# Attention and mixture-of-experts layer on one core: the two halves of the score banks in opposite phase, and each engine's order rearranged around it

## The reference, cut to what matters

```python
h = layernorm(x)
q, k, v = heads(h @ Wq + bq), heads(h @ Wk + bk), heads(h @ Wv + bv)      # 16 heads of 8
y  = softmax(causal(q k^T / sqrt(8))) v
qc = heads(h @ Wcq + bcq); kc, vc = heads(ctx @ Wck + bck), heads(ctx @ Wcv + bcv)
y += softmax(qc kc^T / sqrt(8)) vc
x  = x + y @ Wp + bp
f = layernorm(x)
shared = (silu(f @ w1.T) * (f @ w2.T)) @ w3s.T                             # hidden 512
gates  = sigmoid(f @ router.T), kept for the 2 largest of score + bias, of 8 experts
routed = sum over experts of gate * (silu(f @ a_e.T) * (f @ b_e.T)) @ w3_e.T   # hidden 128 each
out = x + shared + routed
```

## Time and profile before

| | |
|---|---|
| median of 3 runs | 439.8 us (433.45, 439.8, 442.03) |
| the profiled execution, its own time | 441.91 us |
| its span, first to last instruction | 440.2 us |
| TensorE busy | 396.3 us (90%) |
| VectorE busy | 353.5 us (80%) |
| ScalarE busy | 196.4 us (45%) |
| GpSimd busy | 77.8 us (18%) |
| TensorE clock granted, mean | 0.969 |

### The profile page before, as it was taken

One profiled execution on the slowest core, in us unless ns is written; L12 is line 12 of the kernel. 1 busy time (PEld: TensorE's weight loads), 2 busy tenths in 40 slices (PEclk: granted clock), 3 DMA queues, 4 the chain that ended last, 5 costly groups with the idle time before them and its releaser, 6 DMA issues.

```text
span 440.2 us, 10391 instructions
## 1 busy us (share of the span) xinstructions
PE 396.3 (90%) x3735; PEld 295.5 (67%) x3735; DVE 353.5 (80%) x1186; ACT 196.4 (45%) x326; POOL 77.8 (18%) x139
## 2 busy tenths in 40 slices
PE   0569998999989999999999999999989999998986
PEld 0447665666767676777677676767677766765985
DVE  4477776655889889897898888997989889884877
ACT  5135554432544544445534554455443554455221
POOL 4011001300221120311032022212031003201110
PEclk9999999755999999999999999999999999999999
DMA  5621102100021102011111102110101101000000
GB/s 135 211 99 47 61 14 75 54 19 18 20 67 37 50 20 83 12 42 48 46 38 54 48 6 77 42 36 24 72 6 52 43 27 48 1 24 1 2 13 12
DMA packets 28479, 19.63 MB, mean 45 GB/s; under 512 B 6681, under 2 KB 26273, under 8 KB 28449
## 3 DMA queue, kind: packets, MB, share of 16 engines
q1 hardware_dynamic: 27296, 19.02, 13.2%
q10 hardware_dynamic: 1152, 0.20, 0.3%
HBM read 5.58 MB, written 1.05 MB: 15 GB/s over the span
## 4 chain that ended last, share of the span: by engine, by line
PE 51%; DVE 29%; ACT 9%; issue 7%; DMA 1%; SPq 1%; DVEq 0%; POOL 0%; POOLq 0%; ACTq 0%
DVE masked_s L1045 9%; PE Y L579 9%; PE Bk L431 9%; PE Cb L431 7%; ACT probs L804 5%; PE S L455 4%; PE A L431 4%; DVE act L926 3%; DVE shifts L1051 3%; PE S L473 3%; PE Y L546 3%; DVE acc L966 2%; PE S L431 2%; PE Cb L662 2%; DVE qs L1018 2%
## 5 line engine op out<-in xcount | busy, mean ns | idle before, releaser
L804 ACT ACTIVATE probs<-S 128x1024 f32<-128x1024 f32 (+1 forms) x128 | 111.7, 917 | 47.2 <-PE S L457 46.2
L1045 DVE CUSTOM_DVE_ANT_0 masked_s<-S,later_keys 128x256 f32<-128x256 f32 (+1 forms) x256 | 74.1, 353 | 5.0 <-PE S L469 4.8
L1051 DVE TENSOR_REDUCE shifts<-S 128x4 f32<-128x1024 f32 x64 | 75.4, 1218 | 2.4 <-PE S L473 2.0
L791 ACT COPY yT<-Y 128x256 f32<-128x256 f32 x64 | 23.8, 373 | 119.8 <-PE Y L579 119.8
L579 PE MATMUL Y<-probs,vs 128*32 128x256 f32 (+1 forms) x1024 | 65.2, 375 | 5.2 <-DVE qs L1018 3.2
L1100 POOL TENSOR_SCALAR_AFFINE_SELECT probs<-probs 128x1024 f32<-128x1024 f32 x32 | 35.2, 1100 | 152.8 <-ACT probs L804 152.8
L455 PE MATMUL S<-qs,qk 32*128 32x256 f32 x256 | 44.8, 396 | 6.9 <-DVE shifts L1045 5.4
L431 PEld LDWEIGHTS Bk<-w3T,hid 128*128 128x128 f32 x336 | 41.2, 193 | 13.0 <-DVE hid L935 11.4
L431 PE MATMUL Bk<-w3T,hid 128*128 128x128 f32 x336 | 48.8, 289 | 0.6 <-DVE hid L935 0.6
L579 PEld LDWEIGHTS Y<-probs,vs 128*32 128x32 f32 x1024 | 27.6, 113 | 29.1 <-DVE qs L1018 12.5
L926 DVE SCALAR_TENSOR_TENSOR act<-th,A 128x512 f32<-128x512 f32 x42 | 28.6, 682 | 16.7 <-ACT th L784 15.6
(11 more groups left out here) (148 smaller groups left out, 683.2 us busy)
## 6 DMA issues: line engine op xcount, KB each, us to landing
qk<-nat SPq DMA_DIRECT2D x192, 64.0 KB, 1.9
xin<-in_x_dram SPq DMA_DIRECT2D x8, 128.0 KB, 2.3
w_raw<-in_L_ffn_w_dram SPq DMA_DIRECT2D x4, 256.0 KB
xres<-in_x_dram SPq DMA_DIRECT2D x8, 128.0 KB, 2.3
out_dram<-acc SPq DMA_DIRECT2D x8, 128.0 KB, 1.8
cin<-in_ctx_dram SPq DMA_DIRECT2D x8, 64.0 KB, 2.0
w_raw<-in_L_ffn_shared_w_dram SPq DMA_DIRECT2D x4, 128.0 KB
w_raw<-in_L_ffn_w_dram SPq DMA_DIRECT2D x1, 512.0 KB
```

The lines of the kernel that those rows point to most:

```text
L804: nc.scalar.activation(probs[s % 2][:, hs, 0:kept(s)], S[:, hs, 0:kept(s)], ACT.Exp, scale=SCALE).then_inc(exped[s], 1)
L1045: r_ = nc.vector.tensor_tensor_reduce(out=masked_s[:, j, T - q * T:T - q * T + keys], in0=S[:, j, T - q * T:T - q * T + keys], in1=later_k ...
L1051: nc.vector.tensor_reduce(dst.rearrange("p q j -> p j q"), S[:, hs, :].rearrange("p j (q k) -> p j q k", q=NT), AX_X, ALU.max).then_inc(re ...
```

## The change

The second half of `S` runs half a slot behind the first. In the first part of slot s, half 0 gets the exp scores of unit s while half 1 gets the bare scores of unit s+1 (it was s+2); in the second part half 0 gets the bare scores of unit s+2 and half 1 the exp scores of unit s. The bare scores of half 1 wait for the exponential of the slot before. The order of TensorE, ScalarE and VectorE is rewritten for it. GpSimd's `rstd` of the first layer norm moves from slot 6 to slot 5, VectorE's two parts of that layer norm from slots 6 and 7 to slots 4 and 5, the context transpose `cT` from the late to the early job of slot 4. The order of the two uses of `Y` is reversed in slots 4 and 7. In front of the second half's exp scores the fills of `WARM_EXP` are left out.

```diff
-EARLY = [("xT", 1), ("tokens3", -1), ("yT", -1), ("vc", 0), None, ("v", 1), ("qkc", 1), ("tokens0", 0)]
-LATE = [("tokens2", -1), ("qk", 1), ("out", -1), ("x2T", -1), ("cT", 1), ("route", -1), None, ("tokens1", 0)]
+EARLY = [("xT", 1), ("tokens3", -1), ("yT", -1), ("vc", 0), ("cT", 1), ("v", 1), ("qkc", 1), ("tokens0", 0)]
+LATE = [("tokens2", -1), ("qk", 1), ("out", -1), ("x2T", -1), None, ("route", -1), None, ("tokens1", 0)]
...
# TensorE
-            def exp_pass(turn, s):
+            def exp_pass(turn, s, half):
...
+                    keep_warm(turn, s, {} if half else WARM_EXP)
...
             def maxima(turn, s, half):
-                u, o = max_pass(s)
+                u, o = shift_of(s) if half else max_pass(s)
...
-                    if turn.has(0):
-                        wait(pe, exped[s], turn.n(0, half + 1, 2))
...
+                    if half == 0:
+                        if turn.has(0):
+                            wait(pe, exped[s], turn.n(0, 1, 2))
...
+                    elif s > 0 and turn.has(0):
+                        wait(pe, exped[s - 1], turn.n(0, 2, 2))
+                    elif s == 0 and turn.has(-1):
+                        wait(pe, exped[UNITS - 1], turn.n(-1, 2, 2))
...
                 for s in range(SLOTS):
-                    exp_pass(turn, s)
+                    exp_pass(turn, s, 0)
+                    maxima(turn, s, 1)
                     if pair_of(s):
                         if h1_of(s) and turn.has(h1_of(s)[1]):
                             hidden(turn, h1_of(s), 0)
-                        bank_c(turn, EARLY[s])
+                        if s not in (0, 2):
+                            bank_c(turn, EARLY[s])
                         if turn.has(pair_of(s)[1]):
                             hidden(turn, pair_of(s), 1)
+                        if s == 0:
+                            bank_c(turn, EARLY[s])
+                        if turn.at(0):
+                            for i in raw_banks(s):
+                                raw_bank(i)
                         shift_rows(turn, s)
-                        for half in range(2):
-                            maxima(turn, s, half)
+                        if s == 2:
+                            bank_c(turn, EARLY[s])
+                    else:
+                        values(turn, s)
+                        if turn.has(h1_of(s)[1]):
+                            hidden(turn, h1_of(s), 0)
...
+                        shift_rows(turn, s)
+                        bank_c(turn, EARLY[s])
+                    maxima(turn, s, 0)
+                    exp_pass(turn, s, 1)
+                    if pair_of(s):
                         values(turn, s)
                         if turn.has(pair_of(s)[1]):
                             w3_product(turn, pair_of(s))
...
                     bank_c(turn, LATE[s])
# ScalarE
+                    exponential(turn, s, 0)
+                    if not pair_of(s):
+                        values(turn, s)
                     if h1_of(s) and turn.has(h1_of(s)[1]):
                         tanh_h1(turn, h1_of(s))
...
+                    exponential(turn, s, 1)
+                    if pair_of(s):
+                        values(turn, s)
                     from_bank_c(turn, LATE[s])
# VectorE
+                    reduce_half(turn, s, 1)
+                    if s in (3, 5):
                         from_bank_c(turn, EARLY[s])
...
+                    if here:
                         activate(turn, pr)
+                    if s == 1:
+                        from_bank_c(turn, EARLY[s])
+                    if s == 2:
+                        from_bank_c(turn, LATE[1])
...
+                    reduce_half(turn, s, 0)
+                    if s in (4, 6):
                         from_bank_c(turn, EARLY[s])
+                    if s == 4 and turn.has(2):
+                        wait(dve, x_in, turn.n(2, 16, 16))
+                        normalise(turn, 2, ln1, 0, 6, xin, stats1, mv1, xn, rstd1_ready, rstd1, True)
...
+                    if here:
                         add_up(turn, pr)
...
+                    if s == 5 and turn.has(2):
                         wait(dve, xT_ps, turn.n(1))
                         normalise(turn, 2, ln1, 0, 6, xin, stats1, mv1, xn, rstd1_ready, rstd1, False)
-                    if s != 3:
+                    if s not in (1, 3):
                         from_bank_c(turn, LATE[s])
```

More of the change, by code:

```diff
@@ L791, in values, with exponential @@
                     nc.scalar.copy(yT[:, u, :], Y[:, :]).then_inc(yT_ready[u], 1)
+            def exponential(turn, s, half):
+                if turn.has(0):
+                    hs = slice(2 * half, 2 * half + 2)
+                    wait(act, scores[s], turn.n(0, 3 + half, 4))
+                    if half == 0:
+                        v, o = values_of(s - 1) if s > 0 else (SLOTS - 2, -1)
+                        wait(act, valued[v], turn.n(o if s != 1 else -1))
+                    nc.scalar.activation(probs[s % 2][:, hs, 0:kept(s)], S[:, hs, 0:kept(s)], ACT.Exp,
+                                         scale=SCALE).then_inc(exped[s], 1)
@@ L999, in _, with reduce_half @@
             dve.wait_ge(w_bias_in, 16 * 8)
+            def reduce_half(turn, s, half):
+                u, o = shift_of(s) if half else max_pass(s)
+                if not turn.has(o):
+                    return
+                hs = slice(2 * half, 2 * half + 2)
+                if u < NG:
+                    wait_apart(dve, scores[u], turn.n(o, half + 1, 4), dve_passed)
+                else:
+                    wait(dve, scores[u], turn.n(o, half + 1, 4))
+                if turn.at(-1) and u == 0 and half == 0:
+                    dve.wait_ge(consts, 5)
+                dst = shifts[:, :, :].rearrange("p q (j r) -> p q j r", r=QUAD)[:, :, hs, ONE]
+                if u < NG:
+                    for k in range(2):
+                        for q in (1, 0):
+                            keys = T if q else P
+                            j = 2 * half + k
+                            r_ = nc.vector.tensor_tensor_reduce(
+                                out=masked_s[:, j, T - q * T:T - q * T + keys], in0=S[:, j, T - q * T:T - q * T + keys],
+                                in1=later_keys[:, T - keys:T], scale=1.0, scalar=MASKED,
+                                op0=ALU.add, op1=ALU.max, accum_out=dst[:, q, k:k + 1])
+                    r_.then_inc(reduced[u], 1)
+                else:
+                    nc.vector.tensor_reduce(dst.rearrange("p q j -> p j q"),
+                                            S[:, hs, :].rearrange("p j (q k) -> p j q k", q=NT),
+                                            AX_X, ALU.max).then_inc(reduced[u], 1)
@@ L1004, in one_turn @@
-                    if not late:
+                    pr = pair_of(s)
+                    here = pr and turn.has(pr[1])
+                    reduce_half(turn, s, 1)
+                    if s in (3, 5):
                         from_bank_c(turn, EARLY[s])
-                    pr = pair_of(s)
-                    if s == 6 and turn.has(2):
-                        wait(dve, x_in, turn.n(2, 16, 16))
-                        normalise(turn, 2, ln1, 0, 6, xin, stats1, mv1, xn, rstd1_ready, rstd1, True)
```

126 lines of the change are left out of this document (44 added, 82 removed).

## The result

The changed kernel takes 484.7 us (median of 5 runs, 481.85 to 489.9) against 439.38 us of the kernel before: a ratio of 1.107 (95% interval 1.099 to 1.114), 10.7% slower. The medians take in every execution; the ratio leaves out the slow ones, those over 1.5% above the fastest of the same kernel. The prediction of 445 us, and its range, were wrong.

A forecast was written before the change was run, and what follows sets the result against it. No single engine was taken as the bound, but hand-overs between nearly balanced TensorE and VectorE; 3.9 us over six turns, 0.6 for turns 0 and 1 and the last turn's late exponential made 5.3 us more: 445 us, range 438 to 448.5.

The forecast's parts named there:

- The schedule by hand: Loop turns: slot-by-slot sum of the loop through the engines, 48.65 us against 48.0 before, 3.9 us more over six turns.
- The waits named for slots 2 and 5: TensorE waits about 1.1 us at `yT` in slot 2 and about 1.2 us before slot 5's exp scores.
- The late `activate`: VectorE, slot 6 and its like in slots 2 and 5: the 1.36 us wait for ScalarE's tanh goes.
- The mixed block of scores: TensorE, 16 a turn: exp scores beside bare scores take 0.65 us, bounded by 0.59 and about 0.9 us.
- the clock term: Turn 1: keeping the clock makes 445 into 437 us, stretching the half clock costs some us more; clock kept 0.10.
- break every number: Loop turns: a granted clock below 1.00 there would invalidate all the forecast's numbers; no size given.
- TensorE's packed stream: TensorE's work in a loop turn without waits: falls from some 44.2 us to 43.2 us.
- The loop costs more than I charge: Rival, every slot: engines wait for each other, 0.2 us more a slot, turn 50.2 us, about 455 us; chance 0.33.
- The halves cover each other: Rival, loop turns: each slot takes only its fuller engine's need, 45.6 us a turn, 425 us; chance 0.22.
- the phases would drift together again: Rival, loop turns: strict order lets the late half hold the other, turn stays 48 us, 440 us; within the forecast's 0.35.

The follow-up runs named there:

- a_burst: Changed kernel plus 24 constant matmuls before the first exp scores of slot 2 of turn 0; 472.1 us.
- a_holes: Changed kernel plus constant matmuls before the exp scores of slot 5 (10) and slot 0 (5), from turn 2 on; 475.9 us.
- a_warm: Changed kernel plus constant matmuls alone: 24 in turn 0, 8 and 8 in turn 1's slots 0 to 3, 10 in slot 5, 5 in slot 0; 453.0 us.
- a_full: Changed kernel plus constant matmuls in turns 0, 1 and the loop, and three VectorE jobs moved in slots 2 and 3; 443.6 us once, 454 to 459 us three times.

## Why the prediction was wrong

**The schedule by hand held, in part by luck.** It gave 48.65 us for a loop turn; the changed kernel's turns at full clock took 48.8 to 49.1 us. For the whole order it gave 5.3 us. Measured with the clock held are the start (1.0), turns 2 to 6 (4.2) and the end (1.1): 6.3 us, and turns 0 and 1 come on top, where the prediction had 0.6. The waits named for slots 2 and 5 stood where they were put. The late `activate` of the earlier trace rows went, as forecast (17.3 us of waiting for the tanh before, 3.5 us after, over the run).

**Terms inside it were off and cancelled.** The mixed block of scores was taken at 0.65 us, with 0.59 as the low bound; it took 0.44. That bound came from blocks of one kind. The Trainium skill's page TensorE: Matmul & The Clock Gate (The mechanism) says that tiles in different row groups overlap, weight loads included; I used the half of it that speaks of strict order, and the trace now agrees with the other half too. On the other side, the second norm's scaling grew from 0.6 to 1.37 us. The Trainium skill's page SBUF — State Buffer (Who interferes with whom) says that VectorE's `tensor_scalar` can take, in a two-port mode, a pair of ports that it shares with GpSimd, and that whoever comes first holds it for the whole instruction. The row agrees: of two equal operations the second, which began 0.09 us behind GpSimd's mask, took 1118 ns instead of 341 and ended 0.08 us behind the mask's end. The prediction asked when the mask would be late for its reader, not what it would meet. It could have seen it in the trace of the kernel before, where the same scaling of the first norm, beside a GpSimd memset, took 2.22 us for two:

```profile
5.61 2.22 DVE L851 TENSOR_SCALAR xn<-xin,mv,rstd 128x128 f32<-128x128 f32 x2 [1.08 <-POOL rstd L1107]
5.78 1.81 POOL L1147 MEMSET vs<- 128x2048 f32 x1
```

With these two sizes put in, eight loops 0.21 us shorter and slot 3 0.8 us longer, the schedule would have given about 47.7 us. So some 1.4 us a turn of other hand-overs were not charged, an estimate that no run takes apart.

**The step that failed is the clock term.** The sum took the clock's stretches as they were: the clock was priced as a rival, for turn 1 alone, either way, and as a matter apart from the order. Turn 0 and the loop stood at nothing; a stretch below full clock in a loop turn was named among the things that would "break every number" and got no price. The runs put 29.1 of the 45.0 us on the clock: 16.9 in turn 0 (a_burst), 10.1 in turns 2 to 6 and 2.1 behind them (a_holes). 6.3 us are the order's. The other 9.6 us, 2.0 in turn 0 and 7.6 in turn 1, no run parts. An estimate: turn 0 lost 16.9 us for 43.8 us at half clock, and at that rate its rise 3.5 us later and the 13.7 us more that turn 1 spent at half clock (41.0 us, 27.3 before) are worth 1.4 and 5.3 us. That makes about 36 us for the clock and 9 for the order, near the 10 of a_warm. The prediction had both numbers in hand and read them as a gain: TensorE's packed stream became shorter, its turn didn't. In the changed kernel TensorE is busy for 42.3 of 49.1 us, before for 45.3 of 48.0, with waits of up to 1.4 us in slots 0, 2 and 5. The start was misread as well: I took 1.00 in the clock line up to 82 us for a fact, and so didn't see that the rise at 37.7 us was an event of turn 0 that the change could lose.

**The other rivals.** "The loop costs more than I charge" gave the right sign, and a little of the size: the order cost about 9 us where 5.3 were charged, but its loop turn of 49.2 us or more didn't come. "The halves cover each other" failed; that slots 2 to 5 are chained through VectorE and `shift_rows` is the likely reason, and after the repairs a turn still takes 47.6 us, not 45.6. That the phases would drift together again is refuted by the 0.01 us between the two kinds of scores.

**What stays open.** Why the clock falls in one turn and not in the next of the same loop, and why turn 0 keeps the high clock in some executions of a_full and loses it in others, isn't settled by these runs; only that the two fills end the stretches in the loop, and that with the burst the clock rose by 41 us, without it at 61 us or later. Nor is it settled whether the shorter stream or the place of its waits brings the clock down, and how turn 1's loss divides. Whether VectorE's other kinds of operation meet GpSimd's was not tried.

## What to carry to other kernels

On TensorE, idle time has a second price: an edit that empties its stream without shortening the turn can cost the clock, so compare busy time per turn before and after, and price the fall from a stretch at half clock in the same kernel (here 2 to 4 us a turn, 17 us in a sparse first turn). When operations are reordered around another engine's long one, list what each will now run beside, not only what it waits for. And to learn what an order is worth, hold the clock with constant matmuls in its waits and compare turns at full clock: here that left about 9 of the 45 us for the order, and three jobs moved on VectorE gave 7.3 us back (450.85 to 443.59 us). The kernel before must be taken with its clock held as well: its profiled execution of 441.9 us holds 27 us at half clock in turn 1, and its best ones take 433 us.

## What the runs showed of the hardware that was not expected

- Exp scores on rows 0 to 63 and bare scores on rows 64 to 127 of the array, 8 matmuls with 8 weight loads, fit in 0.44 us; a block of exp scores alone on all rows took 0.64 us.
- The granted clock of the profile is unknown, not full, ahead of its first change. The length of a plain transpose (128x128, fp32) tells it: 273 ns at 2.4 GHz, 421 ns at 1.2 GHz.
- Two VectorE scalings of 0.34 us each took 1.37 us beside GpSimd's mask of 1.1 us, in six turns of six, and 2.22 us beside a memset of 1.8 us.
- The same kernel can raise its clock at different times: the kernel before at 37.7 us, its variants that are equal up to there at 38 to 53 us.
